# Head of a fused sign-attention and mixture-of-experts kernel: first tile of x in two halves, fewer warming products, turned signs over two banks and two engines

## The reference

```python
def attn(x, bv_q, bv_k, bv_v):
    bq, bk, bv = ste_sign(bv_q), ste_sign(bv_k), ste_sign(bv_v)   # values of sign()
    Q = ste_sign(x * bq)
    K = ste_sign(x * bk)
    V = x * bv
    scores = jnp.einsum('btd,bsd->bts', Q, K) * d ** (-0.5)
    scores = jnp.where(causal, scores, -jnp.inf)
    attn = jnp.where(causal, jax.nn.sigmoid(scores * 4.0), 0.0)
    return jnp.einsum('bts,bsd->btd', attn, V)
x = layernorm(x + attn(x, bv_q, bv_k, bv_v))
x = layernorm(x + moe_top1(x, w_router, w_gate, w_up, w_down))
```

## Time and profile before

| what | value |
|---|---|
| median of three executions | 545.31 us (543.85 to 545.62) |
| the profiled execution | 545.93 us, of which the span of the trace is 543.1 us |
| PE busy in the span | 516.6 us, 95% |
| DVE, ACT, POOL busy | 404.9, 378.9, 377.4 us |
| share of PE in the chain that ended last | 87% |
| first warming product on PE | 3.83 us |
| first scores on PE | 9.65 us |
| first values on PE | 12.46 us |

### The profile page before, as it was taken

The page is one execution under the profiler, slowest core; times in us unless marked ns, Lnnn a source line. Parts: engine busy times, 40 slices in busy tenths (PEclk is TensorE's granted clock), DMA queues, the critical chain, the costliest instruction groups (busy, mean ns, idle before and its releaser), DMA issues.

```text
span 543.1 us, 12159 instructions
## 1 busy us (share of the span) xinstructions
PE 516.6 (95%) x3990; PEld 458.2 (84%) x4028; DVE 404.9 (75%) x1026; ACT 378.9 (70%) x775; POOL 377.4 (69%) x497
## 2 busy tenths in 40 slices
PE   6999999999999999999999989999999999999992
PEld 5889888888888898888888837999998899999981
DVE  3775787885767957878856735888888888888873
ACT  5885968768867869687686523667776767777752
POOL 4646877776878678777777171477677777787776
PEclk9999999999999999999999999999999999999997
DMA  8995332263232253338761016377777666776211
GB/s 252 362 351 183 94 98 61 78 175 100 98 89 84 90 115 100 94 49 263 172 234 56 7 37 163 90 230 216 213 226 221 196 196 200 211 242 194 75 41 49
DMA packets 91902, 81.52 MB, mean 150 GB/s; under 512 B 31626, under 2 KB 83066, under 8 KB 91840
## 3 DMA queue, kind: packets, MB, share of 16 engines
q1 hardware_dynamic: 84848, 66.39, 42.5%
q0 software_dynamic: 6912, 14.30, 7.6%
q10 hardware_dynamic: 80, 0.07, 0.0%
HBM read 44.33 MB, written 37.90 MB: 151 GB/s over the span
## 4 chain that ended last, share of the span: by engine, by line
PE 87%; issue 4%; DVE 3%; POOL 3%; ACT 1%; DMA 1%; ACTq 0%; DVEq 0%; POOLq 0%; SPq 0%
PE ps L918 12%; PE ps L919 11%; PE ps L920 11%; PE ps L894 10%; PE ps L1074 8%; PE ps L1082 7%; PE ps L1075 7%; PE ps L1100 5%; PE ps L1108 3%; PE ps L1047 3%; PE ps L937 2%; PE ps L950 2%; PE ps L1097 1%; PE ps L1099 1%; PE ps L1098 1%
## 5 line engine op out<-in xcount | busy, mean ns | idle before, releaser
L918 PE MATMUL ps<-v_hl,hl_ring 128*128 128x256 f32 x544 | 176.0, 324 | 0.5 <-DVE hl_ring L1170 0.3
L919 PE MATMUL ps<-v_hl,hl_ring 128*128 128x256 f32 x544 | 153.4, 282 | 0.0
L920 PE MATMUL ps<-v_hl,hl_ring 128*128 128x256 f32 x544 | 153.1, 282 | 0.0
L918 PEld LDWEIGHTS ps<-v_hl,hl_ring 128*128 128x128 f32 x544 | 103.3, 190 | 15.9 <-issue 1.4
L1170 DVE TENSOR_TENSOR hl_ring<-ps,hl_ring 128x512 fp32r<-128x512 f32 (+3 forms) x160 | 93.4, 602 | 23.2 <-ACT ps L695 17.4
L919 PEld LDWEIGHTS ps<-v_hl,hl_ring 128*128 128x128 f32 x544 | 103.6, 190 | 2.4
L920 PEld LDWEIGHTS ps<-v_hl,hl_ring 128*128 128x128 f32 x544 | 103.2, 190 | 0.0
L693 ACT ACTIVATE hl_ring<-ps 128x512 fp32r<-128x512 f32 (+3 forms) x160 | 85.8, 536 | 23.1 <-PE ps L894 10.9
L695 ACT ACTIVATE ps<-ps 128x512 f32<-128x512 f32 (+3 forms) x160 | 87.1, 544 | 0.0
L535 POOL DMA_INDIRECT expert_rows<-xrow,slot x64 | 64.5, 1008 | 29.2 <-issue 24.9
L894 PE MATMUL ps<-q_t,k_t 128*128 128x512 bf16 (+3 forms) x285 | 77.7, 346 | 5.9 <-issue 2.4
(11 more groups left out here) (163 smaller groups left out, 1104.9 us busy)
## 6 DMA issues: line engine op xcount, KB each, us to landing
expert_rows<-xs SPq DMA_DIRECT2D x40, 258.0 KB, 6.0
xs<-expert_rows SPq DMA_DIRECT2D x32, 258.0 KB, 2.8
xall<-in_L_attn_x_dram SPq DMA_DIRECT2D x16, 512.0 KB, 5.3
out_dram<-alone SPq DMA_DIRECT2D x16, 512.0 KB
xall<-in_L_ffn_w_gate_dram SPq DMA_DIRECT2D x32, 256.0 KB
xall<-in_L_ffn_w_up_dram SPq DMA_DIRECT2D x32, 256.0 KB
xall<-in_L_ffn_w_down_dram SPq DMA_DIRECT2D x32, 256.0 KB
xs<-expert_rows SPq DMA_DIRECT2D x31, 64.5 KB
```

Of the source, the lines that this page charges most:

```text
L918: mm(o, ah, v_hl[:, 0, j, :], start=(j == 0 and i % 2 == 0), stop=False, skip_group_check=True)
L919: mm(o, ah, v_hl[:, 1, j, :], start=False, stop=False, skip_group_check=True)
L920: last = mm(o, al, v_hl[:, 0, j, :], start=False, stop=(j == GT * g + i), skip_group_check=True)
```

## The change

Six edits, all in the head:

1. x's first group comes in two transfers of 256 KB (`x_half`, then `x_in[0]`), and ACT takes its signs in two halves (`sgn_half`, then `sgn_ready`). POOL's first product waits for the first half alone.
2. The three vector loads move from SP's queue to the front of ACT's list.
3. The signs of the vectors are made by DVE instead of ACT, from two comparisons each: (v > 0) - (v < 0), four DVE instructions for two ACT instructions.
4. 12 warming products stand ahead of the transposes instead of 28.
5. PE turns tile by tile instead of chunk by chunk, chunk 0 into bank `M0` and chunk 1 into `M1`; the first two tiles wait for `sgn_half` alone.
6. ACT copies chunk 0 of `q_t` and makes chunk 0 of `k_t`, DVE does the same with chunk 1; both read PSUM for both. The first scores also wait for `q_first`.

```diff
             load_x(0, 0)
-            sp.dma_start(bv_row[:, :], bv_v.partition_broadcast(P)).then_inc(bv_row_in, 16)
-            for n, v in enumerate((bv_q, bv_k)):
-                sp.dma_start(bvec[:, n, :], ...).then_inc(bvec_in, 16)
+            for h, landed in enumerate((x_half, x_in[0])):
+                src = x[0, h * GQ // 2:(h + 1) * GQ // 2, :].rearrange("(i p) d -> p i d", p=P)
+                sp.dma_start(xall[:, h * GT // 2:(h + 1) * GT // 2, :], src).then_inc(landed, 16)
...
 # GpSimd
-            pool.wait_ge(x_in[0], 16)
+            pool.wait_ge(x_half, 16)
             g_.tensor_tensor(v_f32[:, 0:1, :], xall[:, 0:1, :], bv_row[:, :].unsqueeze(1), ALU.mult)
...
             pool.wait_ge(key_first, 1)
+            pool.wait_ge(x_in[0], 16)
...
 # ScalarE
+            for n, v in enumerate((bv_q, bv_k)):
+                act.dma_start(bvec[:, n, :], ...).then_inc(bvec_in, 16)
+            act.dma_start(bv_row[:, :], bv_v.partition_broadcast(P)).then_inc(bv_row_in, 16)
             act.wait_ge(consts, 11)
             s_.activation(spare[:, :], spare[:, :], ACT.Sigmoid).then_inc(table_ready, 1)
...
-            signs(0, 0)
-            act.wait_ge(bvec_in, 32)
-            s_.activation(bsgn[:, :, :], bvec[:, :, :], ACT.Sign).then_inc(bsgn_ready, 1)
-            act.wait_ge(bv_row_in, 16)
-            s_.activation(bv_row[:, :], bv_row[:, :], ACT.Sign).then_inc(bv_row_ready, 1)
+            for tiles, landed, done in ((slice(0, GT // 2), x_half, sgn_half), (slice(GT // 2, GT), x_in[0], sgn_ready)):
+                act.wait_ge(landed, 16)
+                s_.activation(sgn[:, :, tiles, :]..., xall[:, tiles, :]..., ACT.Sign).then_inc(done, 1)
+            turned = ps[:, M0, :].bitcast(BF16)[:, 0:GQ]
+            act.wait_ge(sgn_turned, 1)
+            s_.activation(q_t[:, 0, 0, :], turned, ACT.Copy).then_inc(q_first, 1)
             act.wait_ge(qksgn_ready, 1)
-            act.wait_ge(qt_ready, 1)
-            s_.activation(k_t[:, 0, 0:GQ], q_t[:, 0, 0, :], ACT.Copy, scale=qk_sgn[:, 0:1]).then_inc(kt_ready, 1)
+            s_.activation(k_t[:, 0, 0:GQ], turned, ACT.Copy, scale=qk_sgn[:, 0:1]).then_inc(kt_ready, 1)
...
 # TensorE
-            keep_warm(28, moving=identb[:, :])
-            turn_signs(0, 0)
+            keep_warm(12, moving=identb[:, :])
+            pe.wait_ge(sgn_half, 1)
+            for i in range(GT):
+                if i == GT // 2:
+                    pe.wait_ge(sgn_ready, 1)
+                for c in range(DC):
+                    turned = nc.tensor.transpose(ps[:, M0 + c, :].bitcast(BF16)[:, i * P:(i + 1) * P], sgn[:, c, i, :], identb[:, :])
+            turned.then_inc(sgn_turned, 1)
...
 # VectorE
+            dve.wait_ge(bvec_in, 32)
+            v_.tensor_scalar(bneg[:, :, :], bvec[:, :, :], 0.0, None, ALU.is_lt).then_inc(bias_step, 1)
+            dve.wait_ge(bias_step, 1)
+            v_.scalar_tensor_tensor(out=bsgn[:, :, :], in0=bvec[:, :, :], scalar=0.0, in1=bneg[:, :, :],
+                                    op0=ALU.is_gt, op1=ALU.subtract).then_inc(bsgn_ready, 1)
+            dve.wait_ge(bv_row_in, 16)
+            v_.tensor_scalar(bv_neg[:, :], bv_row[:, :], 0.0, None, ALU.is_lt).then_inc(bias_step, 1)
+            dve.wait_ge(bias_step, 2)
+            v_.scalar_tensor_tensor(out=bv_row[:, :], in0=bv_row[:, :], scalar=0.0, in1=bv_neg[:, :],
+                                    op0=ALU.is_gt, op1=ALU.subtract).then_inc(bv_row_ready, 1)
...
-            queries(0, 0)
-            dve.wait_ge(qt_ready, 1)
-            v_.tensor_scalar(k_t[:, 1, 0:GQ], q_t[:, 0, 1, :], qk_sgn[:, 1:2], None, ALU.mult).then_inc(key_first, 1)
+            turned = ps[:, M1, :].bitcast(BF16)[:, 0:GQ]
+            dve.wait_ge(sgn_turned, 1)
+            v_.tensor_copy(q_t[:, 0, 1, :], turned).then_inc(qt_ready, 1)
+            v_.tensor_scalar(k_t[:, 1, 0:GQ], turned, qk_sgn[:, 1:2], None, ALU.mult).then_inc(key_first, 1)
```

More of the change, by code:

```diff
@@ L108, in bass_postln_attn_moe_kernel @@
         bsgn = sb("bsgn", [P, 2, DC], F32)
+        bneg = sb("bneg", [P, 2, DC], F32)
         bv_row = sb("bv_row", [P, D], F32)
+        bv_neg = sb("bv_neg", [P, D], F32)
         qk_sgn = sb("qk_sgn", [P, DC], F32)
@@ L171, in bass_postln_attn_moe_kernel @@
         x_in = [sem(f"x_in{q}") for q in range(NG)]
+        x_half = sem("x_half")
         bvec_in = sem("bvec_in")
+        bias_step = sem("bias_step")
+        sgn_half = sem("sgn_half")
+        q_first = sem("q_first")
         bv_row_in = sem("bv_row_in")
@@ L321, in load_x @@
                 sp.dma_start(xall[:, bass.ds(b * (T // P) + GT * q, GT), :], src).then_inc(x_in[q], 16)
-            load_x(0, 0)
-            sp.dma_start(bv_row[:, :], bv_v.partition_broadcast(P)).then_inc(bv_row_in, 16)
-            for n, v in enumerate((bv_q, bv_k)):
-                sp.dma_start(bvec[:, n, :], v.rearrange("(c p) -> p c", p=P),
-                             allow_slow_non_contiguous=True).then_inc(bvec_in, 16)
+            for h, landed in enumerate((x_half, x_in[0])):
+                src = x[0, h * GQ // 2:(h + 1) * GQ // 2, :].rearrange("(i p) d -> p i d", p=P)
+                sp.dma_start(xall[:, h * GT // 2:(h + 1) * GT // 2, :], src).then_inc(landed, 16)
             load_x(0, 1)
@@ L663, in _ @@
             s_ = nc.scalar
+            for n, v in enumerate((bv_q, bv_k)):
+                act.dma_start(bvec[:, n, :], v.rearrange("(c p) -> p c", p=P),
+                              allow_slow_non_contiguous=True).then_inc(bvec_in, 16)
+            act.dma_start(bv_row[:, :], bv_v.partition_broadcast(P)).then_inc(bv_row_in, 16)
             act.wait_ge(consts, 11)
@@ L765, in batch @@
                         high_weights(0, (k - NS + 4) // 2)
-            signs(0, 0)
-            act.wait_ge(bvec_in, 32)
-            s_.activation(bsgn[:, :, :], bvec[:, :, :], ACT.Sign).then_inc(bsgn_ready, 1)
-            act.wait_ge(bv_row_in, 16)
-            s_.activation(bv_row[:, :], bv_row[:, :], ACT.Sign).then_inc(bv_row_ready, 1)
+            for tiles, landed, done in ((slice(0, GT // 2), x_half, sgn_half), (slice(GT // 2, GT), x_in[0], sgn_ready)):
+                act.wait_ge(landed, 16)
+                s_.activation(sgn[:, :, tiles, :].rearrange("p c i d -> p i c d"),
+                              xall[:, tiles, :].rearrange("p i (c d) -> p i c d", d=P), ACT.Sign).then_inc(done, 1)
+            turned = ps[:, M0, :].bitcast(BF16)[:, 0:GQ]
+            act.wait_ge(sgn_turned, 1)
+            s_.activation(q_t[:, 0, 0, :], turned, ACT.Copy).then_inc(q_first, 1)
             act.wait_ge(qksgn_ready, 1)
-            act.wait_ge(qt_ready, 1)
-            s_.activation(k_t[:, 0, 0:GQ], q_t[:, 0, 0, :], ACT.Copy, scale=qk_sgn[:, 0:1]).then_inc(kt_ready, 1)
+            s_.activation(k_t[:, 0, 0:GQ], turned, ACT.Copy, scale=qk_sgn[:, 0:1]).then_inc(kt_ready, 1)
             act.wait_ge(vs_first, 1)
@@ L887, in scores @@
                     if n == 0:
+                        pe.wait_ge(q_first, 1)
                         pe.wait_ge(key_first, 1)
```

## The result

| kernel | median of its runs | ratio to before, 95% interval |
|---|---|---|
| before, 8 runs | 544.97 us (543.85 to 545.62) | |
| changed, 8 runs | 546.50 us (545.38 to 547.13) | 1.0029 (1.0020 to 1.0039) |

A ratio of 1.0029 is 1.6 us more; 1.5 us less was forecast. The first values, forecast at 10.8 us, came at 14.15, and at 12.46 in the kernel before. That is 1.69 us later. Each figure is from one profiled execution, and the difference is as large as that of the medians.

What follows compares the result with a forecast made beforehand. PE's list sets the time once fed, and warming alone bounds the head up to 7.00 us. Values 1.65 us earlier less 0.15 for the clock gives 1.5: 545.31 - 1.5 = 543.8 us, range 542.8 to 545.2.

Steps and rivals of the forecast that it cites:

- The bound of the head: Head up to 7.00 us: bound by PE's 28 warming products alone, since x's signs were done at 5.77.
- Halves of x, their signs, the transposes: Head, ACT and PE: signs done at 4.7 and 5.6 us, transposes at 6.1, turned signs seen at 6.2.
- my signs of being wrong: Listed observations: bv_row past 6.4 or before 5, first signs past 4.7, warming products after DVE's weights, longer PE idling later.
- Vector loads on ScalarE's queue: Head, loads issued by ACT: bv_row lands at 5.8 us, at best 4.4, at worst 6.4.
- Rival B: Vector loads or DVE's instructions late, copy at 7.5 or later, only 0.3 to 0.9 us gained: 544.7; chance 0.14.
- The 6.6 us that the prediction worked out from it for the turned signs: Head: if the vectors' 128 KB delay x's second half, turned signs come at 6.6 us, the sum unchanged.
- DVE's pair and the wait in front: Head, DVE: four sign instructions, 0.9 us from bv_row's landing to the copy, which starts at 6.7.
- Up to the values: From `key_first` to PE's first values: POOL's 1.81 us, then weights 0.67 behind; values at 10.8, 1.65 us earlier.
- The clock: TensorE, around the scores: rise to 2.4 GHz near 8.2 to 9.2 us, costing 0.15 us.
- C: TensorE's clock rises late: 544.7 for a rise at 10.8, a loss from 12.1 on; chance 0.15, of which 0.04 beyond 12.1.
- Behind the head: After the first values: nothing stands at a fixed time, so the head's gain carries through in full.
- the forecast's own case: Whole kernel: bv_row at 5.8, scores at 7.7, values at 10.8, gain 1.0 to 2.0 us, likeliest 543.8; chance 0.60.

Runs made afterwards that it cites:

- seven: The kernel before with 12 warming products instead of 28 ahead of the transposes; ratio to before 1.0023.
- eleven: The kernel before with 12 warming products ahead of the transposes and 28 behind, instead of 28 and 12; ratio to before 0.9997.
- experiment two: The changed kernel with the three vector loads back on SP's queue, behind the halves of x, bv_row first; ratio to before 0.9997.
- twelve: The changed kernel with the transfer into bv_row reading 128 different rows of x instead of one row 128 times; ratio to before 0.9997.
- five: The changed kernel with 50 warming products instead of 12 between the transposes and the scores; ratio to before 1.0013.
- ten: The changed kernel with bv_row on SP's queue behind x's halves, bvec on ScalarE's, and 28 warming products instead of 12 behind the transposes; ratio to before 0.9980.
- four: The kernel before with only the three vector loads moved to the front of ScalarE's list; ratio to before 1.0031.
- six: The changed kernel with bv_row alone back on SP's queue, behind the halves of x, bvec staying on ScalarE's queue; ratio to before 1.0008.
- one: The changed kernel with bv_row issued first on ScalarE's queue, ahead of the two bvec loads; ratio to before 1.0012.
- eight: The changed kernel with bv_row alone on ScalarE's queue and bvec on SP's, behind the halves of x; ratio to before 0.9991.
- thirteen: The changed kernel with SP holding back the second group of x, and all behind it, until bv_row has landed; 542.69 us, ratio to before 0.9963.
- three: The changed kernel with DVE's wait for bv_row and its pair on it moved behind its copy and keys; ratio to before 1.0013.

## Why the prediction was wrong, point by point

- **The bound of the head** ("the warming alone, not x"): wrong. Experiments seven and eleven show that with 16 products fewer in front the copy comes only 0.4 to 0.6 us earlier, since it then waits for bvec, which landed at 6.9 to 7.2. Without these products the time is 0.23% up, and with them behind the transposes it is what it was. ACT's line at 6.96 showed the first: it waited 1.19 us for bvec, and I counted it as hidden.
- **Halves of x, their signs, the transposes**: right in kind, 0.3 us late. Signs done at 5.05 and 5.86 (4.7 and 5.6 said), turned signs seen by ACT at 6.56 (6.2 said). First signs past 4.7 were one of my signs of being wrong. A half of them took 0.63 us where I took 0.53, at most 0.60, and the first half of x came at 4.42; in experiment two, without the moved loads, ACT took it up at 3.91.
- **Vector loads on ScalarE's queue**: the step that failed. I took 5.8 us for bv_row and 6.4 at worst; it landed at 8.4. The bound added what 128 KB cost at 333 GB/s, as if they only had to share. Beside x the repeated row and everything else together moved at 162 GB/s, less than half that rate. Rival B named the place, but with 0.3 to 0.9 us of gain left; there was none, and even without the clock's part the values were 1.12 us later than before. The Trainium skill, "DMA: Bandwidth & Descriptors", section "Issuing engines are not separate DMA queues", says that transfers issued by different engines share the same 16 DMA engines, so that spreading them saves issue time only. The trace of twelve agrees: both queues together moved 353 GB/s, no more than the 362 of SP's queue alone. The 6.6 us that the prediction worked out from it for the turned signs was met (6.56), by luck: bv_row's packets began at about 5.0, when x's halves had all but landed, and what flew beside these was bvec.
- **DVE's pair and the wait in front**: right. From the landing to the copy 0.9 us were said and 0.9 measured (8.44 to 9.32). The copy took 0.42 for 0.35, the keys 0.47 for 0.35.
- **Up to the values**: right but for the clock. POOL's second product ran 1.81, DVE's weights began 0.72 behind its end (0.67 said).
- **The clock**: underrated, at 0.15 us where it cost 0.57. I had it rise near 8.2 to 9.2 with PE kept full from 7.7 on; instead PE was left empty for 2.60 us ahead of the scores, a consequence of the late load. More idle products in that gap brought 2.4 GHz back in five, and for all but the first scores in ten. B and C came together, where I had priced them apart. A gap is not all of it. Of six traces with one of 1.35 us or more ahead of the scores, five have the first scores at 1.2 GHz (the changed kernel, four, six, seven, twelve) and one at 2.4 (two); with no gap there, one, eight and thirteen have them at 1.2 and three at 2.4. Whether the gap or the sum of the work before counts is not told apart, since the products of five and ten add both. The Trainium skill, "TensorE: Matmul & The Clock Gate", section "What's actually happening", says that the number of slow products at the start varies between runs of one kernel. The traces fit it: three and thirteen had the same 32 products and came out at different levels.
- **Behind the head**: right. Over all kernels the time followed the values: 14.38 gave 1.0031, 14.15 gave 1.0029, 12.03 gave 0.9980, 10.76 gave 0.9963. Seven lies off (12.77, 1.0023), and twelve somewhat (13.07, 0.9997 with an interval up to 1.0010); in all the others the interval holds the shift of the values.

With bv_row at 5.4, experiment thirteen is close to the forecast's own case (5.8): scores at 7.58 at the 1.2 GHz level (7.7 said, at that level), values at 10.76 (10.8), and 0.37% less time (0.28% said). There the clock cost nothing: the values began 0.14 us behind the end of DVE's first weights, as in the kernel before. The rest of the sum held; the landing of bv_row was the term that broke it.

**Open:** what in the memory or the engines makes reads of one row slow beside another stream; why the ratio of seven is 1.0023 with values only 0.31 later; and what decides the clock at the start, since one trace per kernel shows one outcome.

## What to carry to other kernels

Move a load, and ask first what will fly beside it: a broadcast read of one row, put next to the bulk loads, can cost both more than its bytes. An in-order engine should wait for a late input only behind everything that does not need it. In this kernel warming products did more in the stretch in which TensorE would be empty right before its work; before taking some away, look for the second-latest input behind them.

## What the runs showed of the hardware

- 128 reads of the same 1 KB beside another stream held the core's transfers at 162 GB/s from 5.5 to 7.0 us; 128 different rows in their place let 353 GB/s through. With the second group of x held back the same broadcast landed 3.5 us after its issue, instead of 6.6.
- Put ahead of x on the same queue, the broadcast made x's halves land 6.0 us after their issue, against 3.7 in the changed kernel, with 47 GB/s for all queues together from 2.5 to 4.5 us.
- x's halves landed 2.9 us after their issue with no other queue in use, and 3.4 with bvec's small packets on ScalarE's queue.
- After 12, 8 and 12 small products from 3.8 us on, PE was at 2.4 GHz for the scores at 7.64 us in one trace and at 1.2 for those at 7.58 in another. After 2.60 us empty it was at 1.2 GHz for the scores, and with 38 more idle products in that gap it was at 2.4.
